# Making one pair's D in every second duo of batch 1 from channel sums that VectorE scans

## The reference

```python
g = group_norm(x)                       # 32 groups of 6 channels, over rows, columns and the group
s = box_sum(g, axis=w, 5)               # zero-padded sliding sums; the window of 1 over rows does nothing
num = box_sum(s * s, axis=c, 20)
d = box_sum(box_sum(g * g, axis=w, 5), axis=c, 20)
denum = d * c1[w]                       # c1 is 5, at the edges of w 4 or 3
out = x + nan_to_num(num / denum, nan=1.0)
```

## Time and profile before

| | |
|---|---|
| median of 3 runs | 400.02 us (396.32 to 400.2) |
| the profiled execution | 401.84 us, its span 400.1 us |
| mean granted TensorE clock | 0.974 of full |
| busy, share of the span | PE 94%, DVE 66%, ACT 69%, POOL 58% |
| chain that ended last | PE 83%, DVE 10%, ACT 2%, DMA 2% |

### The profile page before, as it was taken

The page is one execution under the profiler, slowest core; times in us unless marked ns, Lnnn a source line. Parts: engine busy times, 40 slices in busy tenths (PEclk is TensorE's granted clock), DMA queues, the critical chain, the costliest instruction groups (busy, mean ns, idle before and its releaser), DMA issues.

```text
span 400.1 us, 8055 instructions
## 1 busy us (share of the span) xinstructions
PE 376.7 (94%) x3140; PEld 375.3 (94%) x3140; DVE 265.2 (66%) x552; ACT 276.9 (69%) x368; POOL 233.9 (58%) x150
## 2 busy tenths in 40 slices
PE   1999999999999999999879999999999999999983
PEld 1999998999999999999769999999999999999982
DVE  2999941657679999999885544555545554455545
ACT  1455547999899998996444777667766677666751
POOL 4000053788788888886085676666766667666431
PEclk9999977999999999999989999999999999999998
DMA  8999100388899962222202222222112222222213
GB/s 243 327 328 326 41 0 2 124 246 263 265 283 281 303 212 80 79 81 80 79 2 79 80 81 79 80 80 77 45 43 77 79 80 80 79 81 80 71 43 124
DMA packets 66485, 50.84 MB, mean 127 GB/s; under 512 B 912, under 2 KB 66448, under 8 KB 66448
## 3 DMA queue, kind: packets, MB, share of 16 engines
q1 hardware_dynamic: 66448, 50.34, 40.8%
HBM read 25.17 MB, written 25.17 MB: 126 GB/s over the span
## 4 chain that ended last, share of the span: by engine, by line
PE 83%; DVE 10%; ACT 2%; DMA 2%; issue 2%; DVEq 0%; ACTq 0%
PE N L443 20%; PE U L434 19%; PE D L443 16%; PE S L434 16%; PE N L434 5%; PE S L443 4%; DVE late_triples L575 3%; DMA xs<-x 2%; DVE ratio L639 2%; DVE N L642 2%; DVE ratio L648 1%; ACT q L392 1%; PE D L498 1%; PE U L519 1%; ACT q L398 1%
## 5 line engine op out<-in xcount | busy, mean ns | idle before, releaser
L315 POOL TENSOR_TENSOR xs<-xs,ratio 128x768 f32<-128x768 f32 x63 | 114.5, 1817 | 95.4 <-DVE ratio L648 95.4
L309 POOL TENSOR_TENSOR xc<-xs,mean_c 128x768 f32<-128x768 f32 x64 | 117.2, 1833 | 62.6 <-DVE mean_c L584 47.0
L639 DVE SCALAR_TENSOR_TENSOR ratio<-D,q 128x768 f32<-128x768 f32 x51 | 48.7, 954 | 92.9 <-ACT q L398 92.9
L642 DVE SCALAR_TENSOR_TENSOR N<-N,q 128x768 f32<-128x768 f32 x64 | 61.6, 962 | 8.5 <-PE N L443 4.8
L648 DVE SCALAR_TENSOR_TENSOR ratio<-ratio,N 128x768 f32<-128x768 f32 x64 | 61.0, 954 | 6.8 <-DVE N L642 0.5
L392 ACT ACTIVATE q<-D 128x768 f32<-128x768 f32 x51 | 41.3, 810 | 30.2 <-PE D L443 30.2
L365 ACT ACTIVATE xs<-S 128x768 f32<-128x768 f32 x36 | 29.2, 811 | 42.9 <-PE S L434 42.9
L434 PE MATMUL S<-b,xc 128*128 128x128 f32 x432 | 55.7, 280 | 0.0
L398 ACT ACTIVATE q<-q 128x768 f32<-128x768 f32 x64 | 54.0, 844 | 2.0
L434 PE MATMUL U<-b5d,xs 128*128 128x128 f32 x432 | 54.1, 275 | 0.4 <-ACT xs L349 0.4
L443 PE MATMUL N<-b_r,xs 128*128 128x138 f32 (+2 forms) x384 | 53.7, 290 | 0.0
(11 more groups left out here) (64 smaller groups left out, 389.2 us busy)
## 6 DMA issues: line engine op xcount, KB each, us to landing
out<-xs SPq DMA_DIRECT2D x31, 768.0 KB, 3.8
xs<-x SPq DMA_DIRECT2D x8, 1536.0 KB, 14.8
xs<-x SPq DMA_DIRECT2D x16, 768.0 KB, 5.3
out<-xs SPq DMA_DIRECT2D x2, 384.0 KB, 2.9
```

What stands on the lines that cost most here:

```text
L309: nc.gpsimd.tensor_tensor(pairs(xc[:, n % XC_RING, :]), pairs(x_flat(n)), mean, ALU.subtract)\
L315: nc.gpsimd.tensor_tensor(x_flat(n), x_flat(n), ratio[:, n % RATIO_RING, :], ALU.add)\
L639: nc.vector.scalar_tensor_tensor(t1, in_bank(d_bank(n)), -TINY, pairs(q[:, n % Q_RING, :]), ALU.add, ALU.mult).then_inc(t1_ready, 1)
L642: nc.vector.scalar_tensor_tensor(in_bank(N), in_bank(N), TINY, pairs(q[:, n % Q_RING, :]), ALU.add, ALU.mult).then_inc(t2_ready, 1)
```

## The change

15 duos of batch 1, 35 and every second one after it up to 63 (`summed`), get the D of their second pair in another way. U and D are made as before for the first pair only (`own_pairs`), three matmuls each in place of six, and ScalarE's `square_xc` and `keep_u` take 384 columns in place of 768. For the second pair:

- GpSimd, `normalise(n)`: the centred pair times 1/deviation, into a line with zeros around each row (`padded`, 424 columns).
- ScalarE, `square_line(n)`: its square, into the second bank of U.
- VectorE, `sum_windows(n)`: a scan from the right that restarts every 20 columns (400 columns, into SBUF as `rising`), a scan from the left, in place in PSUM (394), and the sum of both at the right distance, which is the sum over 20 channels (384, `of_20`).
- TensorE, in `sum_d(n)`: one matmul with the 5-wide band `b5d` as the stationary and `of_20` as the moving operand, 384 columns. It sums over w.

TensorE's next U group (`box_u(n+1)`) now waits for `of_20`, since the squares lie in U's bank. There are some single instructions more: three memsets on GpSimd at the change of batch (`clear_sums`), a matmul of 32 columns with the group variances, two small VectorE instructions at duo 30, a ScalarE root of 32 columns, and four small VectorE instructions and two copies at duo 31 (`spread_scale`).

```diff
+            def normalise(n):
+
+                k = nth_summed(n)
+                if k:
+                    pool.wait_ge(squares_ready, k)
+                else:
+                    pool.wait_ge(scale_ready, 1)
+                pool.wait_ge(xc_ready, n + 1)
+                pair = xc_of(n)[:, PCOLS:2 * PCOLS].rearrange("p (r c) -> p r c", r=PAIR)
+                nc.gpsimd.tensor_tensor(rows_of(padded[:, C_LO:PADDED]), pair,
+                                        scale_c.rearrange("p (r c) -> p r c", r=PAIR), ALU.mult)\
+                  .then_inc(scaled_ready, 1)
...
                     pool.wait_ge(mean_ready, 2)
+                    clear_sums()
                 if m < TOTAL:
                     centre(m)
                 finish(n)
+                if summed(n + SQUARE_AHEAD):
+                    normalise(n + SQUARE_AHEAD)
...
+            def square_line(n):
+
+                act.wait_ge(scaled_ready, nth_summed(n) + 1)
+                act.wait_ge(us_ready, n)
+                nc.scalar.activation(squares_ps, padded, ACT.Square).then_inc(squares_ready, 1)
...
                 square_box(n + BOX_AHEAD)
...
+                if summed(n + SQUARE_AHEAD):
+                    square_line(n + SQUARE_AHEAD)
...
-                box5(U, xc2_of(n), b5d).then_inc(u_ready, 1)
+                if summed(n - 1):
+                    pe.wait_ge(of_20_ready, nth_summed(n - 1) + 1)
+                box5(U, xc2_of(n), b5d, own_pairs(n)).then_inc(u_ready, 1)
...
-                box20(d_bank(n), u[:, n % U_RING, :], batch(n)).then_inc(d_ready, 1)
+                mm = box20(d_bank(n), u[:, n % U_RING, :], batch(n), own_pairs(n))
+                if summed(n):
+                    pe.wait_ge(of_20_ready, nth_summed(n) + 1)
+                    mm = nc.tensor.matmul(D[:, 1, 0:PCOLS], b5d[:, :], of_20, start=True, stop=True)
+                mm.then_inc(d_ready, 1)
...
+            def sum_windows(n):
+
+                k = nth_summed(n)
+                dve.wait_ge(squares_ready, k + 1)
+                if k == 0:
+                    dve.wait_ge(bands_ready, 3)
+                link(nc.vector.tensor_tensor_scan(rising[:, 0:LINE][:, ::-1], restart, squares_ps[:, 0:LINE][:, ::-1], 0.0,
+                                                  ALU.mult, ALU.add))
+                before = squares_ps[:, C_WIN - 1:C_WIN - 1 + REACH]
+                link(nc.vector.tensor_tensor_scan(before, before, restart[:, 0:REACH], 0.0, ALU.add, ALU.mult))
+                if k:
+                    dve.wait_ge(d_ready, n - SUMMED_EVERY + 1)
+                nc.vector.tensor_tensor(of_20.rearrange("p (r c) -> p r c", r=PAIR), rows_of(squares_ps[:, C_WIN - 1:PADDED]),
+                                        rows_of(rising), ALU.add).then_inc(of_20_ready, 1)
...
             def quotient(n, before_ratio=None):
 
+                if summed(n + 2):
+                    sum_windows(n + 2)
                 dve.wait_ge(q_ready, n + 1)
```

More of the change, by code:

```diff
@@ L47 @@
 XC2_SLOT, S2_SLOT, LATE_SLOTS = HALF, HALF + 2, 2
+SUM_SLOT = HALF + 4
+FIRST_SUMMED, SUMMED_EVERY = DUOS + 3, 2
+PITCH = C + C_LO
+REACH = PITCH + C
+BLOCKS = (REACH + C_WIN - 1) // C_WIN
+LINE = BLOCKS * C_WIN
+PADDED = PAIR * PITCH + C_WIN
 LOADS = 8
@@ L119, in window_ratio_kernel @@
         offsets_ps = S[:, 1, PCOLS:PCOLS + CHUNKS * COEFS]
+        sums = xs[:, SUM_SLOT * STEP:(SUM_SLOT + 2) * STEP, :].rearrange("p r c -> p (r c)")
+        padded, restart = sums[:, 0:PADDED], sums[:, PADDED:PADDED + LINE]
+        rising, of_20 = sums[:, 1024:1024 + PADDED], sums[:, 1536:1536 + PCOLS]
+        scale_c = sums[:, 2048:2048 + PCOLS]
+        rows_of = lambda line: line[:, 0:PAIR * PITCH].rearrange("p (r c) -> p r c", r=PAIR)[:, :, 0:C]
+        squares_ps = U[:, 1, 0:PADDED]
+        group_var_ps, newton_ps = [stats_ps[1][:, (1 + i) * GROUPS + CHUNKS:(2 + i) * GROUPS + CHUNKS] for i in range(2)]
         loaded0 = [sem(f"loaded0_{j}") for j in range(LOADS)]
@@ L140, in window_ratio_kernel @@
         inv_ready = sem("inv_ready")
+        group_var_ready = sem("group_var_ready")
+        root_ready = sem("root_ready")
+        scale_ready = sem("scale_ready")
+        scaled_ready = sem("scaled_ready")
+        squares_ready = sem("squares_ready")
+        of_20_ready = sem("of_20_ready")
         xc_ready = sem("xc_ready")
@@ L179, in slot, with summed, nth_summed, own_pairs @@
             return t if t < HALF else RAW + t - HALF
+        def summed(n):
+            return FIRST_SUMMED <= n < TOTAL and (n - FIRST_SUMMED) % SUMMED_EVERY == 0
+        def nth_summed(n):
+            return (n - FIRST_SUMMED) // SUMMED_EVERY
+        def own_pairs(n):
+            return 1 if summed(n) else DUO
         def x_rows(n, duos=1):
@@ L424, in _, with box5 @@
                 square_box(n + BOX_AHEAD)
+                if n == VAR_AT:
+                    act.wait_ge(group_var_ready, 1)
+                    nc.scalar.activation(mean_sum[:, :], dev_sum[:, :], ACT.Abs_reciprocal_sqrt).then_inc(root_ready, 1)
+                if summed(n + SQUARE_AHEAD):
+                    square_line(n + SQUARE_AHEAD)
         @block.tensor
         def _(pe):
-            def box5(bank, rows, weights):
-                for i in range(DUO):
+            def box5(bank, rows, weights, own=DUO):
+                for i in range(own):
                     for j in range(CHUNKS):
@@ L436, in box5, with box20 @@
                 return mm
-            def box20(bank, data, b):
-                for i in range(DUO):
+            def box20(bank, data, b, own=DUO):
+                for i in range(own):
                     for j, (first, end) in enumerate(SPAN):
@@ L513, in average_squares @@
                                           averager[0][:, 0:1], start=True, stop=True)
+                if b:
+                    by_group = ssq_c[:, 0, :].rearrange("p (g c) -> p g c", g=GROUPS)
+                    mm = nc.tensor.matmul(group_var_ps, averager[0][:, :], by_group[:, :, 0], start=True, stop=True)
                 return mm
@@ L691, in _ @@
                     sum_m2(1)
-                quotient(n, before_ratio=spread_late if n == MEAN_AT else scale_late_bands if n == VAR_AT else None)
+                quotient(n, before_ratio=spread_late if n == MEAN_AT else scale_late_bands if n == VAR_AT else
+                         spread_scale if n == VAR_AT + 1 else None)
                 for j in range(len(LATE_SETS)):
```

28 lines of the change are left out of this document (26 added, 2 removed).

## The result

The changed kernel takes 437.05 us (median of 5, 436.68 to 443.48) against 400.02 us (396.32 to 401.78): a ratio of 1.094 with a 95% interval of 1.087 to 1.102 (ratios and intervals here and below go by the single executions, so they aren't quite the quotients of the medians). The profiled execution is the one of 443.48 us, its span 441.7 us; it is 6.4 to 6.8 us above the four others, at a mean granted clock of 0.967 against 0.981.

The account below looks back on a forecast made before the run. TensorE was taken to bound the kernel, with 1.24 us of slack for VectorE. Chain +33.2, clock +16.5 and change of batch -1.5 gave +48 us on the 400.02 us median: 448 us, range 420 to 464.

Parts of the forecast that it names:

- The chain: Batch 1: the new series begins only after GpSimd's addition of duo n-3 and delays TensorE's next even D, 2.21 us per two duos.
- Its length: From one even duo's D to the next: 13.35 us against 11.14, with TensorE standing 2.93 us before each even D.
- The term of +33.2 us: Duos 34 to 62: 2.21 us more for each two duos, 15 times.
- The scans: VectorE's two scans of 400 and 394 columns: 0.95 us each, plus 0.03 behind each, 1.96 in all.
- The upper row: VectorE's scans priced at 0.95 us each, not the 0.58 of one column per step.
- TensorE's saving: TensorE in 15 duos: net 0.72 us less per two duos, 10.8 us in all, lying wholly in the wait.
- The clock: TensorE's clock falls after the new 2.93 us waits: 1.1 us each, between 0 and 1.8, +16.5 us in all.
- The change of batch: Three memsets delay GpSimd's centring of duo 32, while VectorE's instructions get through earlier: -1.5 us, between -3 and +1.
- The signs named: Profile after: first 200 us unchanged, 2.9 us waits before even D, TensorE about 85%, scans near 0.95 us, waits through all engines.
- the 440 to 455 that had the highest chance: Whole kernel's time: the forecast's own band, 440 to 455 us, chance 0.40.
- the rival of scans at a column per step with the loss of clock: VectorE's scans take 0.58 us, period 12.61, TensorE's clock still loses 1.1 a wait: +37, 437 us; fast scans' chance 0.17.
- the clock holds: TensorE's clock loses nothing after the new waits, everything else as forecast: +31.7, 432 us; chance 0.18.

Follow-up runs that it names:

- The first experiment: Changed kernel with GpSimd's `normalise` of duo n+3 moved ahead of the addition of duo n; 392.37 us, 0.986 of the kernel before.
- The second experiment: Changed kernel with the three U and three D matmuls of each summed duo's first pair done twice on TensorE; 436.45 us.
- the two kernels with the same chain and filled waits: Changed kernel with each summed duo's first-pair U and D matmuls done twice, 436.45 us; changed kernel with its S group done twice, 433.86 us.
- the kernel without scans: Changed kernel with both scans replaced by ordinary multiplications of the same operands and lengths, channel sums left out; 434.82 us, 436.7 us a second time.
- the kernel with both orders: Changed kernel with `normalise` first in GpSimd's turn and `square_line` ahead of ScalarE's square of S; 388.67 us, 0.974 of the kernel before.

## Why the prediction was right, step by step

- **The chain.** That the new series starts only behind the addition of duo n-3, and that its end holds up TensorE's next even D, was right, and it decided the result. The first experiment shows it alone: one line moved, 45 us.
- **Its length.** Predicted 13.35, measured 13.58 us; TensorE's wait in it predicted 2.93, measured 2.95. By parts, predicted and measured: to GpSimd free 8.30 and 8.37 (the first group behind a wait takes 1.69, not 1.61); `normalise` with its hand-over 1.00 and 1.04; the square 0.54 and 0.56; the scans 1.96 and 2.04; the sum 0.47 and 0.47; product and start of TensorE 1.08 and 1.10. The term of +33.2 us should have been +36.6.
- **The scans.** 0.987 and 0.985 us for 400 and 394 columns, against 0.57 for a multiplication of that length. The upper row was the right choice (0.95). The rate that the Trainium skill states in "DVE: opcode table, instruction layouts, handler registers and perf-mode slots", section 6, Datapath and trigger behaviour, is half of the ordinary one. The traces agree: (987 - 571) ns for 400 columns is 1.04 ns more for each, and a column of an ordinary instruction costs (954 - 484) / (768 - 312) = 1.03 ns by the earlier trace rows.
- **TensorE's saving.** Predicted 0.72 us a pair, wholly in the wait. The matmul of 384 columns takes 0.65 us from its start to the next group's (311.08 to 311.73), and the period at which TensorE is the bound is 10.39 us, so the saving is 0.75. The second experiment shows that it was worth nothing.
- **The clock: the term that was mis-sized.** Predicted +16.5 us, 1.1 for each of 15 waits. In the profiled execution it was 6.3 us: 1.47 to 1.63 us behind each of four waits, all among the first five, and nothing behind the other eleven. So a fall costs more than the 1.1, near the upper bound of 1.8, and the step that was wrong is the count, from "both waits of this kind before were followed by half clock" to "so are most of the waits of 2.93 us". For the four other executions no profile places the clock. They stand 3.3 to 4.2 us above the fastest executions of the two kernels with the same chain and filled waits (433.37 us at a clock of 0.993, 432.9 at 0.994), so the clock can have cost them some 4 us in all, wherever it fell. But the kernel before has such a cost too: its median of 400.02 is 3.7 us above its fastest execution of 396.32. Between the medians the two nearly cancel, which is luck: 36.6 us of chain leave 0.4 of the 37.0 for the clock and the change of batch together, where 15.0 were predicted. In the kernel without scans, with a wait of only 2.12 us, the clock fell behind about every second one, all the way. So the length of a wait alone doesn't decide; what does stays open, and I couldn't have read it from two waits.
- **The change of batch.** Predicted -1.5, bounds -3 and +1. From the averaging of the means (L585) to D of duo 31 the profiled execution took 211.08 - 193.91 = 17.17 us, before it was 212.66 - 196.78 = 15.88: +1.3, just outside the bounds, with the clock at half for a longer stretch (201 to 210 us, where before it was at half twice for 3 to 4 us). In the kernel with both orders, which has the same code here, the clock fell only once (198 to 202 us), and it took 209.99 - 196.72 = 13.27. The mechanism was as predicted (L684 0.35 in place of 1.75 us); in the changed kernel the wait for the centring, 2.88 us, took the place of the one for the ratio.

- **The signs named.** The waits of 2.9 us, the 85% and scans near 0.95 us came as forecast. The chain of waits doesn't go round through the root, VectorE and the scans, as was forecast: that view stays on GpSimd's queue. And the first 200 us weren't as before in the profile: D of duo 31 began 1.58 us earlier, although the change of batch took 1.3 us longer. The 2.9 us gained ahead of it fit the clock, which had been at half for some 4 us near the start of the execution in place of 11. From D of duo 31 to D of duo 62 it was 43.2 us longer (36.5 of chain, 6.6 on top), which with this makes up the 41.6 us between the spans.

The predicted 448 us was 11 too high: 3.4 too little for the chain, 14.6 too much for the clock and the change of batch together. It also lay outside the 440 to 455 that had the highest chance, though inside the range. The number nearest to the measured one, 437 us, stood with the rival of scans at a column per step with the loss of clock, and only by luck: its scans of 0.58 us took 0.987, and its 16.5 us of clock weren't lost. The rival whose mechanism is nearest is "the clock holds", 432 us, or 435 with the chain as measured.

## What to carry to other kernels

When a change adds a series of steps over several engines whose queues are written by hand, walk it through the queues in order and note at each what stands ahead of it and when that is released; the start of the series, and not the work in it, decided between 437 and 389 us here. A piece that has its input early goes ahead of whatever waits for a late one. And where an engine waits in front of a step that is on the chain, its saving is nothing, while work put into that wait is free (1.4 us a pair of duos here) and, for TensorE, may even pay, as in the kernel without scans.

## What was not expected

- The kernel without scans became 13 us faster with six more matmuls in each pair of duos (from 436.7 to 423.4 us), because TensorE's clock no longer fell to half. A wait of 2.12 us brought that on about every second time, a wait of 2.95 us at a longer period four times in fifteen in the one profile, and not once in the last ten.
- The times of one kernel go with the clock: in the three series of the experiments the kernel before took 396.0 to 396.7 us in runs with a mean granted clock of 0.990 or 0.991, 398.2 to 400.2 with 0.983 to 0.986, and 401.5 to 402.0 with 0.974 to 0.979. A gain of 1% is hidden in that.
- A group of TensorE right behind a wait takes 1.68 us in place of 1.61, even at full clock.
- One execution took 2241.8 us, with a mean granted clock recorded as 1.00 and every group of matmuls more than five times as long (up to 9.20 us for six, in place of 1.61). It came once in the runs of this study.
